# The last attention written out for all 24 heads, its surplus maxima dropped, its turn a plain product, and the output projection in the same program

## The reference

```python
qkv = imagelike_bhwc @ qkv_w + qkv_b             # b = 2 images, n = 48 * 48 = 2304 tokens
q, k, v = ...                                     # each (b * 12 heads, 2304, 16)
attn = jnp.einsum('bqd,bkd->bqk', q * scale, k)
rel_h = jnp.einsum('bhwc,hkc->bhwk', r_q, Rh)
rel_w = jnp.einsum('bhwc,wkc->bhwk', r_q, Rw)
bias = (rel_h[:, :, :, :, None] + rel_w[:, :, :, None, :]).reshape(b * nh, n, n)
attn = jax.nn.softmax(attn + bias, axis=-1)
out = jnp.einsum('bqk,bkd->bqd', attn, v)
return out @ proj_w + proj_b
...
x = x + _L3_conv_ref(_gn(x), ...)
```

## Time and profile before

| | us |
|---|---|
| median of 3 runs | 4721.52 (4720.76 to 4724.44) |
| the profiled execution's own time | 4717.87 |
| its span in the trace | 4716.0 |

### The profile page before, as it was taken

How to read it: one execution, slowest core, us unless ns; L and a number is a source line. 1 busy time by engine, 2 the same in 40 slices (tenths; PEclk the granted TensorE clock), 3 DMA queues, 4 the chain that set the end, 5 groups by cost and what they waited for, 6 DMA issues and landing times. The chain is left out here.

```text
span 4716.0 us, 120406 instructions
## 1 busy us (share of the span) xinstructions
PE 3464.0 (73%) x47313; PEld 1758.2 (37%) x47313; DVE 3572.9 (76%) x3605; ACT 2692.4 (57%) x4414; POOL 1536.5 (33%) x1124
## 2 busy tenths in 40 slices
PE   3898764148777756306777775765999999999996
PEld 2476622012222223101222222451566665666563
DVE  2755455869999936677999993555888888888884
ACT  0366617735555532864545542141888888888883
POOL 0122200059999920007999990000000000000000
PEclk8899977558888878656878887865999999999998
DMA  3433212432222220232222212133112222211213
GB/s 85 97 68 65 39 42 62 120 94 68 61 65 68 57 66 17 89 118 76 71 61 63 65 48 64 59 120 91 52 52 60 57 56 54 55 52 52 52 53 88
DMA packets 165533, 316.14 MB, mean 67 GB/s; under 512 B 71035, under 2 KB 110147, under 8 KB 161392
## 3 DMA queue, kind: packets, MB, share of 16 engines
q1 hardware_dynamic: 164976, 308.38, 24.9%
HBM read 199.70 MB, written 108.02 MB: 65 GB/s over the span
## 5 line engine op out<-in xcount | busy, mean ns | idle before, releaser
L2005 DVE TENSOR_REDUCE l3a_mx<-l3a_mx 128x2 f32<-128x768 f32 x1362 | 1223.9, 951 | 201.9 <-PE l3a_mx L1909 195.5
L1981 ACT ACTIVATE l3a_p<-l3a_s 128x384 f32<-128x384 f32 x2592 | 1158.5, 491 | 159.7 <-PE l3a_s L1931 149.6
L1398 POOL TENSOR_TENSOR l_scan_sc<-l_scan_s,l_scan_repc 128x768 f32<-128x768 f32 x576 | 1032.3, 1840 | 5.8 <-DVE l_scan_s L1376 5.7
L1335 ACT ACTIVATE l_scan_da<-l_scan_da,l_scan_a 128x768 f32<-128x768 f32 x576 | 504.0, 875 | 637.0 <-PE l_scan_da L1259 636.8
L1931 PE MATMUL l3a_s<-l3a_q,l3a_k 125*32 125x384 f16 x10368 | 827.7, 327 | 3.3 <-issue 3.3
L1909 PE MATMUL l3a_mx<-l3a_k,l3a_q 124*32 124x384 f16 x10896 | 717.0, 335 | 36.3 <-DVE l3a_mx L2005 29.4
L1259 PE MATMUL l_scan_dup<-l_scan_du,l_scan_pick 96*128 96x512 bf16 (+1 forms) x1152 | 350.7, 393 | 367.4 <-DMA l_scan_dt<-l_dtp 213.3
L1943 PE MATMUL l3a_o<-l3a_p,l3a_vh 128*32 128x288 f32 x6920 | 579.5, 406 | 3.0 <-issue 2.9
L1389 POOL TENSOR_TENSOR l_scan_bup<-l_scan_dus,l_scan_repb 128x768 f32<-128x768 f32 x192 | 353.1, 1839 | 656.6 <-DMA l_scan_repc<-l_bcp 656.6
L1875 POOL TENSOR_TENSOR l3a_norm<-l3a_out,l3a_spread 128x576 f32<-128x576 f32 x25 | 35.9, 1434 | 1366.8 <-DMA l3a_spread<-l_inverses 1366.8
L1286 PE MATMUL l_scan_y<-l_scan_sc,l_scan_sum 128*32 128x256 f32 x3456 | 450.1, 475 | 10.4 <-POOL l_scan_sc L1398 10.3
(11 more groups left out here) (197 smaller groups left out, 4242.6 us busy)
## 6 DMA issues: line engine op xcount, KB each, us to landing
l3a_q<-l_qx SPq DMA_DIRECT2D x104, 486.0 KB
l_scan_du<-l_dup SPq DMA_DIRECT2D x144, 144.0 KB, 2.8
l_scan_dt<-l_dtp SPq DMA_DIRECT2D x144, 144.0 KB, 3.4
l_scan_repb<-l_bcp SPq DMA_DIRECT2D x48, 384.0 KB
l_scan_repc<-l_bcp SPq DMA_DIRECT2D x48, 384.0 KB
l3a_q<-l_hx SPq DMA_DIRECT2D x26, 288.0 KB
l_dtp<-l_prep_high_t SPq DMA_DIRECT2D x16, 432.0 KB, 3.1
l_dup<-l_prep_high_u SPq DMA_DIRECT2D x16, 432.0 KB, 3.1
```

Source lines behind the costliest of these rows:

```text
L1335: act.activation(da_ps[st % 2][:, 0:TC], da_ps[st % 2][:, 0:TC], ACT.Exp, scale=A[:, column:column + 1]).then_inc(exped, 1)
L1398: pool.tensor_tensor(SC[:, st % NSC, :], S[:, n, :], REPC[k % 2][:], ALU.mult).then_inc(weighted, 1)
L1981: act.activation(P[:, k % NP, third * SW:(third + 1) * SW], s_ps[g % NS_PS][:, 0:SW], ACT.Exp)\
L2005: dve.tensor_reduce(MX[:, h % NB, qt, 2 * pair:2 * pair + 2], mx_ps[bank][:, :, 0:RG], AX_X, ALU.max)\
```

## The change

`layer3_attention` is written out for all 24 heads without a loop, and every wait is on a constant. The order of scores, passes and values within a head stays. It differs in this:
- Passes exist for real heads only (1296 reductions). The last pass of all is the turn of head 23; the last 126 units have none. There are no loads for heads that don't exist, and no round before the first head.
- The four clearing matmuls are gone. TensorE's first wait is still for all of `consts`; the waits for a head's loads stand before its first pass.
- The turn is `pe.matmul(out[0:KT, 0, 0:128], M[:], eye[:, :])` in place of `pe.transpose` with the same operands.
- SP loads the places of a buffer next to its head, keys at unit 2 of a head ahead of the stores of sums, and stores the result before the third copy of the queries.
- The projection is in the same block. Its weights are loaded at the start. Its operand for image 0 is loaded into a tile `OT0` at heads 7 and 13, the first half of image 1 at head 22 into the tile of V, once V is copied for the last head, and the second half behind the last head's result. There are 20 pieces (five of each image's half, the fifth of 256 tokens), in the two PSUM buffers of the passes. VectorE adds two pieces, then makes the last inverses, then adds the rest. SP stores the pieces after the last load.

```diff
-        ring = [("mx", u) for u in range(NMX)]
-        ring.insert(TURN_AT, ("turn", None))
...
-        def before_loop():
-
-            for h in range(2):
-                for slot in range(UPH if h == 0 else AHEAD):
...
+        passes, at_unit = [], {}
+        turn_of, joins = {}, {}
+        def place(unit, what):
+            at_unit.setdefault(max(unit, -1), []).append(len(passes))
+            passes.append(what)
+        for m in range(BH * NMX + TURN_LATER + 1):
+            unit = m // 3 * CYC + MX_AT[m % 3] - UPH - AHEAD
+            h, lag = divmod(m - NMX, NMX)
+            if h >= 0 and lag == JOIN_LATER:
+                joins[len(passes)] = h
+            if h >= 0 and lag == TURN_LATER:
+                turn_of[h] = len(passes)
+                place(unit, ("turn", h))
+            if m < BH * NMX:
+                place(unit, ("mx", m))
+        joins.setdefault(turn_of[BH - 1], BH - 1)
...
+        def operand(b, c):
+            return OT0[:, c, :] if b == 0 else V_FLAT[0:CP, c * L:(c + 1) * L]
+        def load_operand(sp, b, c):
+            head = b * NH + c * HPC
+            sp.wait_ge(out_stored, (head + HPC) * STORES)
+            if b == 1:
+                sp.wait_ge(v_ready[(BH - 1) % NB], (BH - 1) // NB + 1)
+            sp.dma_start(operand(b, c), o_dram[head:head + HPC, :, :].rearrange("h d l -> (h d) l"))\
+              .then_inc(ot_loaded[b][c], 16)
+        operand_at = {HPC + 1: (0, 0), NH + 1: (0, 1), BH - 2: (1, 0)}
+        pieces = [(b, m, at, w) for b in range(B) for at, w in LCH for m in range(CC)]
+        def accumulator(n):
+            return mx_ps[n // 2 % NR][0:CP, n % 2, :]
...
-                for i in range(NB):
-                    sp.dma_start(K[i][3 * HD:KROWS, :], t["l3_places"]).then_inc(consts, 16)
-                sp.wait_ge(mx_taken, NX + TURN_AT + 1 + LEAD)
                 load_shift(sp, 0)
-                with sp.Fori(0, NI) as i:
-                    for e in range(HPB):
...
+                    if h in operand_at:
+                        load_operand(sp, *operand_at[h])
+                    queries(3)
+                    if h + 1 < BH:
+                        load_shift(sp, h + 1)
+                store_sums(sp, BH - 1)
+                store_inverses(sp, BH - 1)
+                store_out(sp, BH - 1)
+                load_operand(sp, 1, 1)
+                for n, (b, m, at, w) in enumerate(pieces):
+                    sp.wait_ge(added, n + 1)
+                    where = slice(b * L + at, b * L + at + w)
+                    sp.dma_start(out[m * CP:(m + 1) * CP, where], X[:, m, where]).then_inc(x_stored, 16)
+                sp.wait_ge(x_stored, 16 * len(pieces))
...
-                    if what[0] == "turn":
-                        pe.transpose(out[0:KT, 0, 0:128], M[:], eye[:, :]).then_inc(mx_made, 1)
...
+                    if what == "turn":
+                        pe.wait_ge(m_made, i + 1)
+                        pe.matmul(out[0:KT, 0, 0:128], M[:], eye[:, :], start=True, stop=True).then_inc(mx_made, 1)
+                        return
...
-                for g in range(4):
-                    pe.matmul(o_ps[32 * g:32 * g + 32, 0:QG], VH[NB - 1][:, 0, :], P[:, 0, 0:QG], start=True, stop=False)
-                pe.wait_ge(loaded[0], LOADS)
-                pe.wait_ge(loaded[1], LOADS)
...
-                with pe.Fori(0, NI) as i:
-                    for g in range(ST):
-                        score(i, g)
-                        maxima(i, g)
-                        for e, k in values_at(g):
-                            values(i, e, k)
+                for n in at_unit[-1]:
+                    mx_pass(n)
+                for u in range(NU):
+                    score(u)
+                    for n in at_unit.get(u, []):
+                        mx_pass(n)
+                    for k in values_at(u):
+                        values(k)
+                values(BH * KPH - 1)
+                pe.wait_ge(w_loaded, 32)
+                pe.wait_ge(mx_taken, len(passes))
+                for n, (b, m, at, w) in enumerate(pieces):
+                    if m == 0 and at == 0:
+                        for c in range(CC):
+                            pe.wait_ge(ot_loaded[b][c], 16)
+                    since(pe, added, n - 3)
+                    for c in range(CC):
+                        mm = pe.matmul(accumulator(n)[:, 0:w], w_sb[:, c, m * CP:(m + 1) * CP],
+                                       operand(b, c)[:, at:at + w], start=c == 0, stop=c == CC - 1)
+                    mm.then_inc(projected, 1)
...
+                def add(n):
+                    b, m, at, w = pieces[n]
+                    x = X[:, m, b * L + at:b * L + at + w]
+                    dve.wait_ge(projected, n + 1)
+                    dve.scalar_tensor_tensor(x, accumulator(n)[:, 0:w], b_sb[:, m:m + 1], x, ALU.add, ALU.add)\
+                       .then_inc(added, 1)
+                dve.wait_ge(w_loaded, 32)
+                for n in range(2):
+                    add(n)
+                invert(BH - 1)
+                for n in range(2, len(pieces)):
+                    add(n)
+                dve.wait_ge(added, len(pieces))
...
-        with Scope(nc, "l3o") as so:
-            OT = so.sb("ot", [CP, CC, TOK])
...
-            out_projection(nc, "l3p", X, OT, t["l3_pwT"], t["l3_pb"], CP, CC, l3_rows, out)
```

More of the change, by code:

```diff
@@ L1847, in _ @@
[L1847 to L1854 removed]
+                        load_queries(sp, h, v)
@@ L1913, in maxima, with mx_pass @@
-                def maxima(i, g):
-                    for h, pos, what in stream(g):
-                        if pos == 0:
-                            pe.wait_ge(loaded[h % NB], i * (PB * LOADS) + (h // NB + 1) * LOADS)
-                        if what[0] == "turn":
-                            pe.wait_ge(m_made, i * HPB + (h + LEAD))
-                        mx_pass(i * (HPB * NX) + (h * NX + pos), h, (h + pos) % NR, what)
-                def score(i, g):
-                    e, x = divmod(g, UPH)
+                def mx_pass(n):
+                    what, i = passes[n]
+                    since(pe, mx_taken, n + 1 - NR)
+                    out = mx_ps[n % NR]
+                    if what == "turn":
+                        pe.wait_ge(m_made, i + 1)
+                        pe.matmul(out[0:KT, 0, 0:128], M[:], eye[:, :], start=True, stop=True).then_inc(mx_made, 1)
+                        return
+                    h, x = divmod(i, NMX)
+                    if x == 0:
+                        pe.wait_ge(loaded[h % NB], (h // NB + 1) * LOADS)
+                    qt, pair = divmod(x, MPQ)
+                    for a in range(2):
+                        g = 2 * pair + a
+                        for c in range(4):
+                            at = qt * 128 + 32 * c
+                            mm = pe.matmul(out[32 * c:32 * c + 32, a, 0:RG], Q[h % NB][0:KROWS - 1, variant(g), at:at + 32],
+                                           K[h % NB][0:KROWS - 1, g * RG:(g + 1) * RG], start=True, stop=True)
+                    mm.then_inc(mx_made, 1)
@@ L1923, in score @@
+                def score(u):
+                    h, x = divmod(u, UPH)
                     k, third = divmod(x, THIRDS)
```

347 lines of the change are left out of this document (147 added, 200 removed).

## The result

The changed kernel takes 4658.8 us (median of 4 runs, 4654.22 to 4665.78), the kernel before 4721.1 us on the same chip (4 runs, 4717.48 to 4724.44): a ratio of 0.9869 with an interval of 0.9852 to 0.9887, some 62 us. The forecast was 4676.5 us with a range of 4668 to 4692.

What follows compares the result with a forecast made beforehand. TensorE's array was taken to bound the steady part, a chain the end. Gains of 0.9 + 5.0 + 12 + 28 - 1 = 45 us took the 4721.5 us median to 4676.5 us, range 4668 to 4692.

Steps and rivals of the forecast that it cites:

- Register operations: Last attention's steady part: removing them gains 0, hidden by TensorE's busy array; bounds 0 to 2 us.
- Rival D: Written-out last attention: instructions come late, 76 us more, 4752.5 us in all; chance 4%.
- Loop boundary: Jump back in the last attention's loop: unrolling saves 5.0 us, at least 3.3.
- Surplus maxima: Last 126 units after the last real turn: without 66 unneeded passes, 0.41 us a unit, gain 12 us (7 to 15).
- Rival A: Last head: TensorE's short waits lower its clock, 0.48 us a unit, gain 4 instead of 12, 4684.5 us; chance 15%.
- Tail: Last copy to the end: projection inside the program, one last load instead of four, gain 28 us (22 to 30).
- half-clock loss: Second image's projection matmuls: TensorE returns from idle at clock 0.51 for 6 records, 2.6 us more.
- Rival B: Tail: ten stores share engines with the last load, landing up to 7 us later, gain 21, 4683.5 us; chance 11%.
- Rival C: Last head: handovers set the pace, so removing passes gains nothing, 0.51 us a unit, 4688.5 us; chance 5%.
- The turn: One matmul per head as a product instead of a transpose: taken as 0, other bound 4 us lost.
- operand loads: Projection operand loads at heads 7, 13 and 22: hidden, 1 us lost for a held-up instruction load, bounds 0 to 5.
- Start: Before the first maxima: four clearing matmuls gone, 0.9 us saved; TensorE's wait for all three places copies taken as 0.

Runs made afterwards that it cites:

- padded kernel: Changed kernel with extra long-met constant waits on TensorE, one ahead of each score and values pass, two ahead of each maxima pass: 4704.5 us, ratio 0.9975.
- experiment 7: Changed kernel with 66 surplus maxima passes put back, on tiles already loaded and with unused results: 4669.7 us, ratio 0.9898.
- experiment 8: Changed kernel with the output projection as a program of its own behind the attention again: 4678.5 us, ratio 0.9914.
- experiment 9: Changed kernel with the turn as a transpose of all columns again, in place of the product of 18: 4654.1 us, ratio 0.9873.

## Why the prediction was wrong

- **Register operations: the failed step.** "In the steady part TensorE's array is busy without a gap, so this hides them: 0", with 2 us as the upper bound. The array's busy share answers another question. The operations cost no array time, but they add 3567 instructions to the 50857 of TensorE's stream between turns 2 and 24 (7%). With them the blocks of instructions land 2.1 us ahead of their use in the median, not 4.4, and at some blocks the array stands idle for 1 to 3 us. Measured: 13 us between turns 2 and 24, the rest of the 18.0. The row that should have warned was there: waits on issue in the looped attention. That they were not only at the jump, a list of the turns all through the stage shows; 11 of 22 spacings were too long, and the bound would have been 15.6 us.
- **Rival D, the same mechanism with the wrong sign.** It took the first attention's 22.1 us of issue waits for a mark of written-out code. That stage has 57.5 records of TensorE per us from 200 to 577 us, the last attention 44.5 looped and 42.2 written out. Its waits are of the same kind: numbered from 200 us on, 17 of the 18 gaps of over 0.9 us in the kernel before stand at 114 or 115 modulo 256. So they go with a dense stream (no run varied that stage), and writing out with constants makes the last attention's stream less dense. The Trainium skill (Runtime: NRT & Kernel Launch, section "Instruction fetch mechanics") says that the cost of crossing a block of 16 KB is mostly hidden and that branches break the prefetch. The jump's wait of 3.25 us agrees; the straight stretches of the looped body, and the padded kernel without any jump, show block crossings that are not hidden.
- **Loop boundary: right.** 5.0 forecast; 59.67 us across it before, 54.65 us in the written-out kernel. The sum took it whole; the wait of 3.25 us is one part of it, the 3.4 us at half clock behind the wait another, which the prediction didn't name.
- **Surplus maxima: right.** 12 forecast, 12.9 between the two kernels, 11.9 in experiment 7. The choice of 0.41 us a unit between 0.386 and 0.45 was good: 51.78 / 126 = 0.411. It was a choice, and in part luck: that figure holds the copies at the half ends, for which the sum had another 0.9 us, and the long runs go at 0.395.
- **Rival A: out.** The granted clock is 1.00 in the last head although TensorE's weight loads waited 82 times for ScalarE there, 23.0 us in all (engine and line, releaser, us, times, longest):

```profile
PEld l3a_s L1937 <- ACT l3a_p L1990: 23.0, 82, 0.6
```

  The Trainium skill (TensorE: Matmul & The Clock Gate, section "A second HAM failure mode: psum-queue depth-cycling") says that frequent micro-idles between groups of matmuls make the clock oscillate. This head doesn't show it: the weight loads wait, but the array is busy for 50.02 of 52 us, and the clock stays.
- **Tail: right.** 28 forecast, 27.6 measured, 28.0 in experiment 8. The half-clock loss was put at 2.6 us and is 3.4 (8 records, not 6). **Rival B: out**, the stores began 0.4 us behind the load and didn't delay it: 6.0 us as forecast.
- **Rival C: out**, by 12.9 us.
- **The turn and the operand loads.** The turn was right at nothing (experiment 9). The 1 us put down for a held-up instruction load can't be told apart in 1205 us.
- **Start: 1.2 for 0.9.** That the first maxima still wait for all places was stated and its price not asked for: 13.6 us were to be had there.
- **The rest**, 2.8 us, lies before the attention, in code that the change doesn't touch.

The range failed because the term of the register operations, costed at nothing, had a bound of 2 us where the trace allowed 15.6. With the 13 us the forecast would have been 4663.5 us, 5 us from the result; 2.8 of these lie before the attention and are luck of the two traces.

## What to carry to other kernels

Count the instructions of each engine's stream, register operations and extra waits included. "The array is busy, so it hides them" holds only if the instructions also arrive in time, and waits on issue in straight code say that they may not; whether the stalls stand a fixed number of instructions apart settles it. Before costing a loop's control at nothing, list the distances of one recurring operation over the whole stage: what repeats at the same places in the code goes, or comes, with the code. Where an engine's first wait is for several transfers, ask which of them the first instruction needs.

## What the runs showed of the hardware

- Straight code can be short of instructions. With some 50850 instructions of TensorE in 1205 us (42.2 per us) it lost 0.3 to 2.6 us; with 53980 to 55209 it lost 15 to 32 us, whether the extra ones were register operations or waits. The stalls stand at multiples of 256 instructions, the boundaries of 16 KB blocks, and nearly all end 1.2 to 1.7 us behind the landing of a block, whose transfer takes 1.1 us in the median. The median block landed 4.4 us ahead of its use in the changed kernel, 1.9 to 2.3 us in those with more instructions. Why some blocks come late and others not is open.
- Waits that were long met are not always free: with some 200 more of them in a head, an undisturbed head went from 54.65 to 55.4 us. With some 140 more, none of them ahead of the maxima, it stayed at 54.65.
- A stall of some 3 us can cost more than its length: behind the jump's (3.25 us) the granted clock was 0.50 for 3.4 us.
- The last attention begins at another time in each build and trace: from 3202.2 to 3220.6 us over fifteen profiles, with nothing changed ahead of it (3214.4 and 3208.9 in the two of the kernel before). Whole times of two kernels differ by that as well, which is why the verdicts above go by segments counted from a point inside the stage.
- Seven matmuls in a pause of 6 us kept the granted clock at 1.00; without them it was 0.50 for the first 8 records behind it, which cost 3.4 us.
